# Idle products, weight splits and a gather in new places in the early blocks of a gated attention and mixture-of-experts kernel; its last two scatter-adds made independent

## The reference

```python
x = x + tanh(g_xattn[0]) * xattn(layernorm(x), ctx, ctx)   # sigmoid(Q^T K / sqrt(256)), times V
# ffn(layernorm(x)), per row:
t = xf * rsqrt(mean(xf * xf) + EPS) * norm_w
logits = t @ gate_w.T + gate_b
vals, idx = top_k(logits, 4)
gates_k = softmax(vals)
h = einsum('mh,eoh->emo', t, w1) + b1
a = minimum(h[..., ::2], 7.0);  b = clip(h[..., 1::2], -7.0, 7.0)
act = a * sigmoid(1.702 * a) * (b + 1.0)
y = einsum('emi,edi->emd', act, w2) + b2
x = x + tanh(g_ffn[0]) * (layernorm(x) + sum over the four experts of gates_k * y)
```

## Time and profile before

| what | us |
|---|---|
| median of 3 runs | 883.6 |
| lowest and highest run | 882.62, 885.98 |
| the profiled execution, its own time | 880.83 |
| its span, first to last instruction | 879.1 |
| PE busy in the span | 830.2 (94%) |
| DVE busy | 583.0 (66%) |
| POOL busy | 511.1 (58%) |
| ACT busy | 318.1 (36%) |
| mean granted TensorE clock (1 is full) | 0.985 |

### The profile page before, as it was taken

The page is one execution under the profiler, slowest core; times in us unless marked ns, Lnnn a source line. Parts: engine busy times, 40 slices in busy tenths (PEclk is TensorE's granted clock), DMA queues, the critical chain, the costliest instruction groups (busy, mean ns, idle before and its releaser), DMA issues. The chain is left out here.

```text
span 879.1 us, 14603 instructions
## 1 busy us (share of the span) xinstructions
PE 830.2 (94%) x3820; PEld 639.0 (73%) x3821; DVE 583.0 (66%) x1123; ACT 318.1 (36%) x460; POOL 511.1 (58%) x534
## 2 busy tenths in 40 slices
PE   5998899888799999999999999999999999999993
PEld 2554455666688888888888888888888888888882
DVE  4555665785478687767768777685766767685551
ACT  4455575431243334233333433232332423232120
POOL 0033346754566667656666667575665756676553
PEclk9999999899999999999999999999999999999997
DMA  6643666324577576537657757464553737433332
GB/s 196 215 142 122 195 213 214 120 84 145 119 215 204 156 181 165 136 92 192 154 144 201 218 128 209 82 198 96 146 147 72 213 69 219 85 87 60 60 61 36
DMA packets 50965, 127.24 MB, mean 145 GB/s; under 512 B 8256, under 2 KB 12352, under 8 KB 50944
## 3 DMA queue, kind: packets, MB, share of 16 engines
q1 hardware_dynamic: 31792, 86.83, 29.8%
q0 software_dynamic: 19152, 40.19, 24.8%
HBM read 96.25 MB, written 30.74 MB: 144 GB/s over the span
## 5 line engine op out<-in xcount | busy, mean ns | idle before, releaser
L478 POOL TENSOR_SCALAR y_out<-y_sb,add_gate 128x512 f32<-128x512 f32 x76 | 161.1, 2120 | 20.5 <-DVE y_sb L919 18.8
L628 ACT ACTIVATE ht_hi<-bank 128x512 fp32r<-128x512 f32 x75 | 44.9, 598 | 353.6 <-PE bank L1140 341.7
L482 POOL DMA_INDIRECT out_rows<-y_out,add_idx x76 | 125.0, 1645 | 66.2 <-issue 40.9
L462 POOL DMA_INDIRECT xg<-t_rows,gather_idx x72 | 84.8, 1178 | 75.1 <-issue 41.2
L429 POOL DMA_INDIRECT list_rows<-entry,place x64 | 64.7, 1011 | 108.6 <-DVE place L830 91.3
L1164 PE MATMUL bank<-w_hi_even,xt_hi 128*128 128x512 f32 x312 | 125.2, 401 | 2.8 <-DVE xt_lo L906 2.8
L1164 PE MATMUL bank<-w_hi_even,xt_lo 128*128 128x512 f32 x312 | 122.5, 393 | 0.0
L1164 PE MATMUL bank<-w_lo_even,xt_hi 128*128 128x512 f32 x312 | 121.5, 389 | 0.0
L912 DVE TENSOR_TENSOR ht_lo<-bank,ht_hi 128x512 fp32r<-128x512 f32 x75 | 51.9, 692 | 102.3 <-ACT ht_hi L628 101.3
L1164 PE MATMUL bank<-w_hi_odd,xt_hi 128*128 128x512 f32 x288 | 115.4, 401 | 0.0
L1164 PE MATMUL bank<-w_hi_odd,xt_lo 128*128 128x512 f32 x288 | 113.1, 393 | 0.0
(11 more groups left out here) (162 smaller groups left out, 1676.7 us busy)
## 6 DMA issues: line engine op xcount, KB each, us to landing
raw<-in_w SPq DMA_DIRECT2D x96, 512.0 KB
bias<-in_b SPq DMA_DIRECT2D x16, 768.0 KB
k_sb<-in_ctx SPq DMA_DIRECT2D x8, 512.0 KB, 3.8
v_sb<-in_ctx_t SPq DMA_DIRECT2D x8, 512.0 KB
t_rows<-t_sb SPq DMA_DIRECT2D x8, 512.0 KB
out_rows<-base SPq DMA_DIRECT2D x8, 512.0 KB
x_sb<-in_x SPq DMA_DIRECT2D x7, 512.0 KB
t_rows<-zeros SPq DMA_DIRECT2D x1, 1792.0 KB, 8.3
```

What stands on the lines that cost most here:

```text
L462: pool.indirect_dma_start(out=xg[:].bitcast(F32), out_offset=None, in_=t_rows, in_offset=bass.IndirectOffsetOnAxis(ap=gather_idx[:], axis= ...
L478: pool.tensor_scalar(y_out[:], y_sb[:], add_gate[:, 0:1], None, ALU.mult).then_inc(yo_ready, 1)
L482: pool.indirect_dma_start(out=out, out_offset=bass.IndirectOffsetOnAxis(ap=add_idx[:], axis=0), in_=y_out[:], in_offset=None, compute_op=A ...
L628: act.activation(ht_hi[:].rearrange("p k t -> p (k t)"), ps_h[:], ACT.Copy).then_inc(ht_hi_ready, 1)
```

## The change

In the code of before, with the names above:

- **Spare rows.** `t_rows` and the output get 256 spare rows where they had 128; the pads of lists in even and in odd columns name different ones. The two transfers that zero them in round 0 are 256 KB longer each.
- **Block table.** Three maxima on `n_f` become one, against a table `least` of 16 small memsets at the start. It holds 4 for expert 0, 2 for expert 1 and, new, 2 for the last expert. The last expert has some five blocks in this data, so the number of blocks stays.
- **Splits.** In rounds 5, 6 and 7 ACT splits the weights before it makes the base rows. DVE's rests of pieces 4 and 5 move from behind block 0's linear rows to behind `enter(B - 3)`.
- **Sixth block.** POOL issues `gather(5)`, the rows of the sixth block, ahead of `add_rows(2)`. PE turns the block table ahead of block 3's linear product, and DVE copies it ahead of that block's linear rows.
- **Idle products.** 4 become 9 and 5 become 6 around `turn_t(B - 1)`; 4 each are new at three places; at the end 7 and 7 become 2 and 6.
- **Last scatter-add.** ACT multiplies the last block by its gate into a tile of its own, with index and gate copied beforehand, and POOL adds it without waiting for the scatter-add before.

```diff
@@ tables
+            two = pads[:].rearrange("p (c two) w -> p c two w", two=2)
+            dve.tensor_copy(two[:, :, 0, 0], pad_i[:].broadcast_to([P, CAP // 2]))
+            dve.tensor_scalar(two[:, :, 1, 0], pad_i[:].broadcast_to([P, CAP // 2]), float(P), None, ALU.add
+                              ).then_inc(pads_ready, 1)
...
+            for e in range(E):
+                dve.memset(least[:, e:e + 1], {0: 4.0, 1: 2.0, E - 1: 2.0}.get(e, 1.0))
...
-            link(dve.tensor_scalar(n_f[:], n_f[:], 1.0, None, ALU.max))
-            link(dve.tensor_scalar(n_f[:, 0:2], n_f[:, 0:2], 2.0, None, ALU.max))
-            link(dve.tensor_scalar(n_f[:, 0:1], n_f[:, 0:1], 4.0, None, ALU.max))
+            link(dve.tensor_tensor(n_f[:], n_f[:], least[:], ALU.max))
@@ POOL
-            block(0, 0, 3, 2, False, 1)
+            gather(5)
+            add_rows(2)
             last = over_experts(pool, block)
+            final = lists[:, bass.ds(column(last + 1), 1), :].squeeze(1)
+            pool.tensor_copy(last_gate[:], final[:, 1:2]).then_inc(last_set, 1)
+            pool.tensor_copy(last_idx[:], final[:, 0:1]).then_inc(last_set, 1)
             add_rows(last)
-            add_rows(last + 1)
+            pool.wait_ge(last_set, 2)
+            pool.wait_ge(yl_ready, 1)
+            pool.indirect_dma_start(
+                out=out, out_offset=bass.IndirectOffsetOnAxis(ap=last_idx[:], axis=0),
+                in_=y_last[:], in_offset=None, compute_op=ALU.add).then_inc(added, DMA)
@@ ACT
-                base_rows(b - 1)
                 for k in pieces:
                     split_hi(0, 0, k)
+                base_rows(b - 1)
...
             hidden_turned(last)
+            act.wait_ge(last_set, 1)
+            act.wait_ge(y_ready, last + 2)
+            act.activation(y_last[:], y_sb[:], ACT.Copy, scale=last_gate[:, 0:1]).then_inc(yl_ready, 1)
@@ DVE
             enter(B - 3)
+            for k in range(NP1, NPW):
+                split_lo(0, 0, k)
             choose(B - 2, 2 * P, 1)
...
             linear_rows(0, 0)
-            for k in range(NP1, NPW):
-                split_lo(0, 0, k)
...
             gate_rows(3, 0)
-            linear_rows(3, 0)
             dve.wait_ge(col_mm, 1)
             dve.tensor_copy(block_col[0:1, 4:], ps_g[0:1, 3:MAXG]).then_inc(table_ready, 1)
+            linear_rows(3, 0)
@@ PE
             linear_product(0, 0)
-            keep_clock_up(4)
+            keep_clock_up(9)
             turn_t(B - 1)
             router(B - 1)
             turn_rows(1)
-            keep_clock_up(5)
+            keep_clock_up(6)
             gate_product(1, 0)
...
+            keep_clock_up(4)
             pe.wait_ge(hi_ready, NPW)
             pe.wait_ge(lo_ready, NPW)
             down(0, 0)
...
             down(1, 0)
+            keep_clock_up(4)
             turn_hidden(2)
             turn_rows(3)
+            keep_clock_up(4)
...
             gate_product(3, 0)
-            linear_product(3, 0)
             pe.wait_ge(col_ready, 1)
             pe.matmul(ps_g[0:1, 0:P], col_p[:], ident[:], start=True, stop=True).then_inc(col_mm, 1)
+            linear_product(3, 0)
             turn_rows(4)
 
             last = over_experts(pe, block)
-            keep_clock_up(7)
+            keep_clock_up(2)
             turn_hidden(last)
-            keep_clock_up(7)
+            keep_clock_up(6)
             down(last, (E - 1) % 2)
```

15 lines of the change are left out of this document (10 added, 5 removed).

## The result

| what | before | after |
|---|---|---|
| median, us | 883.6 | 879.46 |
| lowest and highest run | 882.62, 885.98 | 876.27, 879.68 |
| the profiled execution, its own time | 880.83 | 879.68 |
| its span | 879.1 | 877.9 |
| mean granted clock | 0.985 | 0.984 |

The medians differ by 4.1 us. The ratio, which goes by all five runs of each and not by the middle one (their means are 884.25 and 878.71), is 0.9937 after to before, with a 95% interval of 0.9914 to 0.9961: by it the change takes 5.6 us (3.4 to 7.6). The forecast was 9.8. In a second group of runs, made for the experiments, the changed kernel had 878.82 (ratio 0.994, 0.9919 to 0.9961). The direction was right and 4 us of the expected gain are not there. One slow run of the experiments (891.5 us, of early_choose) is left out of its ratio.

The account below looks back on a forecast made before the run. PE, busy 94% of the span, sets the time; gains lie in its idle and low-clock time. -1.2 - 1.5 + 0 - 0.7 - 3.9 + 0.8 + 0.3 - 3.6 = -9.8, 883.6 to 873.8 us; range 868.5 to 878.8.

Parts of the forecast that it names:

- The end: Last block: fewer idle products and no wait for the previous scatter-add start the last one earlier: -3.6 us (-2.6 to -3.9).
- The rounds: Routing rounds 5 to 7: splits ahead of base rows remove PE's two waits for `t_sb`: -1.2 us (0 to -1.3).
- the unplaced wait: DVE's `choose(B - 2)` starts after 6.8 us idle with no releaser; taken as unchanged, 2 us to either side.
- Blocks 0 and 1: Five and one more idle products hold the clock through the router, block 1's gate product earlier: -1.5 us (0 to -1.7).
- Blocks 2 and 3: Eight idle products around `turn_hidden(2)` and `turn_rows(3)` hold the clock in about half the cases: -0.7 us (-1.5 to +0.5).
- What I had said of block 0: Four idle products ahead of `down(0, 0)`: clock gain is lost waiting for block 3's gather; counts 0.
- Block 5: Earlier gather removes block 5's wait, block 6 waits 2.6 us: -3.9; clock may fall behind it +0.8; later waits +0.3.
- +0.3, waits of tenths in the blocks after: Blocks after block 6: POOL has less lead than before, a few waits of tenths: +0.3 us.
- the wait comes back whole: Rival: block 2's scatter-add still lands at 224.1 and the clock falls at block 6; about 876.7 us, chance 0.15.
- the idle products don't do what they are for: Rival: clock low from the transposes on as before, four products in the way at block 3; 876.5 us, chance 0.14.

Follow-up runs that it names:

- early_choose: The changed kernel with the last sequence's choice, weights and places made on DVE ahead of the rest of block 1's rows; 881.13 us, ratio 0.9954 to before.
- tail_only: The kernel before with the end alone: spare rows, one maximum with its table, last scatter-add from ACT's tile, two and six idle products; 881.10 us, ratio 0.9971.
- undo_base: The changed kernel with ACT's base rows ahead of the weight splits again in rounds 5 to 7; 880.15 us, ratio 0.9941 to before.
- after_again: The changed kernel measured once more, as it is, in a second group; 878.82 us, ratio 0.9940 to before.
- lists_first: The changed kernel with SP's third list load (indices of block 1's rows) issued ahead of four weight loads; 879.75 us, ratio 0.9945 to before.
- undo_gather: The changed kernel with block 2's scatter-add ahead of block 5's gather again, the block table still early; 878.71 us, ratio 0.9936 to before.
- pool_first: The changed kernel with the third list load ahead of four weight loads and the first scatter-add (zeros) behind sequence 6's list scatters; 875.44 us, ratio 0.9918.
- undo_idle: The changed kernel with early idle products as before (4 and 5, none at the three new places), the end's kept; 878.39 us, ratio 0.9925 to before.
- pool_first_ug: pool_first with block 2's scatter-add ahead of block 5's gather again; 878.46 us, ratio 0.9928 to before.
- pool_first_again: pool_first, the same kernel, measured once more in a later group; 879.60 us, ratio 0.9928 to before.

## Why the prediction came out 5.7 us low

By the medians it is 5.7 us, 879.46 against 873.8; by the ratio 4.2, a gain of 5.6 against 9.8.

- **The end, -3.6.** Right, and in every trace that has it (626.0 to 622.4). Two scatter-adds 4.1 us apart cost nothing that shows: from the last one's issue to the end of the span it is 9.4 us before and 9.55 after.
- **The rounds, -1.2, and the unplaced wait, 0 with 2 to either side.** T7-t0 is 133.0 on average in the three traces with the base rows first and 131.3 in the eleven with the splits first, these from 128.6 to 133.5. But these 1.7 us are not the term. Cut further, at the transposes of sequences 4 and 6 (T4, T6; both waits of the term lie between them) and at the first product of block 0 (B0), in us:

| traces | T6-T4 | B0-T6 | T7-B0 |
|---|---|---|---|
| before | 36.1 | 13.5 | 8.1 |
| tail_only | 36.1 | 12.1 | 9.6 |
| undo_base | 36.4 | 12.1 | 7.6 |
| eleven with the splits first | 37.1 (34.7 to 38.5) | 11.0 to 11.3 | 7.0 to 8.6 |

Three of the eleven (the changed kernel, after_again, lists_first) have 34.7 to 35.2: there both waits are gone but for 0.3 us at most, and the term is right within 0.3. In the other eight another wait for `t_sb`, of 1.5 to 1.7 us, stands in round 6 or 7, and the mean is 0.9 us longer than with the base rows first, not 1.2 shorter. In undo_gather, ACT starts on a score product after 5.04 us of idling and 2.3 us after PE has ended it, and DVE waits 2.56 us for the root behind it:

```profile
139.08 0.60 ACT L583 ACTIVATE score<-bank 128x512 f32<-128x512 f32 x1 [5.04 <-remote]
```

Whether that belongs to the new order (eight of eleven against none of three) is open. What T7-t0 gained lies behind T6, where the prediction had 0: block 0 starts some 1.1 us earlier in every trace with the splits first than in tail_only and undo_base, the unplaced wait of the trace of before (1.4 us that tail_only, with the same code up to there, doesn't have) is gone, and T7-B0 is over 8 only in the three traces (before, tail_only, undo_gather) in which DVE starts late, after 1.4 to 2.9 us with no releaser in the profile, on the second half of the last sequence.

- **Blocks 0 and 1, -1.5: the first step that failed in the changed kernel's own trace.** I wrote that the gather of block 1's rows comes "some 0.3 us later", and that is so: counted from t0 it goes out at 130.8 before and 131.0 after (163.39 - 32.60, 165.15 - 34.19). But I didn't ask when it lands. It landed 4.8 us later, 168.4 in the times of before. My router ended at 169.2 there, less the 1.2 of the rounds 168.0: no reserve was left, and every microsecond that PE came earlier, as it did by 2.4 when block 0 started sooner (B0-T6, 13.5 to 11.0), turned into a wait. In that wait the clock fell that I had counted as held. R1-t0 is 138.1 on average with the base rows first (three traces) and 137.4 in the eight with the splits first and POOL's queue as it was; R3-t0 is 167.1, 168.8 and 169.6 there, and 165.8, 168.6, 169.8, 170.0 and 170.1 in the changed kernel and those that are the same program up to block 3. Nothing is left at block 3 of this term, or of the 1.7 above. For block 1 the cause is POOL's chain of 21 us, shown by pool_first. For block 3 I have an argument only: the last sequence's choice stands behind block 1's rows on DVE, and POOL's last lists behind the choice.
- **Blocks 2 and 3, -0.7.** 0 by undo_idle, as far as its ratio can tell. That the stretches of half clock would go was right for the profiled execution and not for most others: behind turn_rows(3) the clock fell in eight of ten traces, where I had written "about half of the cases". What I had said of block 0, that what the clock gives back is not kept, was true there too.
- **Block 5, -3.9, +0.8, +0.3.** The pieces up to block 6 came as told: gather issued 1.7 us ahead of the time foreseen, no wait at block 5, 2.94 us at block 6. What failed is "+0.3, waits of tenths in the blocks after". The next wait was whole, 4.20 us with half clock behind it, in three of the eight traces with this order and its loads unheld. In R8-R3 the part gives -2.3 (52.2 against 54.5 on average) or, with the collision, +1.3 (55.8); by the shares seen, about -1 where -2.8 stood.
- **The sum.** -3.6 for the end, about -1 for block 5, and about -1 for all that lies ahead of it, which is what the ratio leaves and no trace shows: -5.6.

Of the rivals, *the wait comes back whole* (876.7) and *the idle products don't do what they are for* (876.5) come nearest in time. Of the first it is right that a wait with half clock behind it came back, but one block later, for another gather, and in three traces of eight. Of the second it is right that the idle products buy nothing that shows. But the clock did hold through transposes and router, in all traces but those of before and tail_only. In pool_first_ug PE runs idle products, transposes, narrow products and transposes again from 162.65 to 168.3, and the clock stays at 1.00, as its window shows:

```profile
166.00:169.00 3.00, 3.00 (x24) 2.87 (x25) 0.00 (x1) 2.85 (x4) 2.39 (x3) 1.00 0.51 111
```

In pool_first, the same code up to there, PE from 162.79 on runs the same products with the same single wait of 0.50 us, and yet the clock falls at 169.1, under the next idle products:

```profile
169.40:172.60 3.20, 3.20 (x9) 2.50 (x8) 2.70 (x16) 1.65 (x4) 2.30 (x3) 0.51 0.81 242
```

The Trainium skill's rule that transposes don't count as busy ("TensorE: Matmul & The Clock Gate", Part 4) is neither shown nor refuted by these traces. The fall in pool_first goes with it; the clock that stayed at 1.00 in pool_first_again and pool_first_ug goes against it. The range left out the median by 0.7 us (by the ratio the time is 878.0 and within it), because I had taken the failures at block 1 and behind block 5 for alternatives, and they come together.

## What to carry to other kernels

When PE gets faster at one place, look up, for each transfer that it will then ask for, the time of its landing and the whole queue of the engine that issues it, back to the last wait in it: if there is none for 20 us, that queue may set the time. Removing a wait for one gather can bring the following gather, scatter-add and loads together; ask for two blocks further on which transfers are then issued in the same microsecond. Work whose inputs are ready (here, a choice that stood 6 us behind another block's rows) belongs into the hole, but measure it: pool_first and the gather's new place each took a wait of 3 to 5 us out of the trace, and the time moved by 1 us or not at all. One trace of a kernel is not its mean: a wait or a stretch of half clock that is gone in one execution was back in another of the same program.

## What was not expected of the hardware

- Waits end late without a cause in the rows. DVE, idle for 2.32 us, reads the rank products 4.2 us after PE's last of them (pool_first_ug); ACT's copy starts 7.1 us after PE's transposes (early_choose), DVE's choice 2.5 us after the router (before). It falls in different places in executions of one program, and T7-t0 of eleven traces scatters by 4.9 us. What it is stays open; I saw no transfer that goes with all of them.
- A gather of 128 rows landed 8.8 us after its issue when a bias load was issued 0.1 us ahead of it, and 4.0 us when that load came 2.1 us behind it. One that was issued 2.1 us behind the first of six weight loads took 7.0.
- A wait of 2.94 us at block 6 was followed by full clock in the trace of the changed kernel, and one of 3.03 us by half clock in after_again, the same program. The two executions of pool_first differ likewise behind turn_rows(1), after a wait of 0.5 us in each.
